# One language-model block on one core: the first sequence's six masked products in one group, its state share behind the turn of v, and GpSimd's copy of x's last columns behind the third addition

## What is computed

```python
h = emb[tokens] * sqrt(192) + position
u = rmsnorm(layernorm(h))
z, xBC, dt = split(u @ in_proj)            # 384, 512 and 24 columns
xBC = silu(conv4(xBC) + conv_b)            # causal, four taps over the tokens, per channel
x, B, C = split(xBC)                       # 384, 64, 64
dt = softplus(dt + dt_bias); decay = exp(-dt * exp(A_log))
S_t = decay_t * S_(t-1) + dt_t * x_t B_t   # per head, a 16 x 64 state
y = S_t C_t + D * x;  y = y * silu(z)
m = y @ out_proj;  v = rmsnorm(m)
h = h + m + (silu(v @ w_gate) * (v @ w_up)) @ w_down
x2 = layernorm(h)                          # the router takes two of eight experts
out = h + shared(x2) + sum_e cw_e * expert_e(x2)
```

## Time and profile before

| | |
|---|---|
| median of 3 runs | 796.38 us (795.68 to 796.73) |
| the profiled execution | 796.69 us, of which the span of the profile is 794.9 us |
| busy: PE, DVE, ACT, POOL | 757.6, 636.5, 546.8, 328.3 us |
| granted clock of PE | 0.991 of full over the span, full in the loop |
| one pass of the loop (first weighed sum of DVE at 389.85, then at 436.43) | 46.58 us |

### The profile page before, as it was taken

The page is one execution under the profiler, slowest core; times in us unless marked ns, Lnnn a source line. Parts: engine busy times, 40 slices in busy tenths (PEclk is TensorE's granted clock), DMA queues, the critical chain, the costliest instruction groups (busy, mean ns, idle before and its releaser), DMA issues.

```text
span 794.9 us, 23059 instructions
## 1 busy us (share of the span) xinstructions
PE 757.6 (95%) x7278; PEld 646.6 (81%) x7278; DVE 636.5 (80%) x1691; ACT 546.8 (69%) x1242; POOL 328.3 (41%) x478
## 2 busy tenths in 40 slices
PE   2679999999999999999999999999999999999897
PEld 1556788988888898888888888888988888888786
DVE  4699987879788787978878797887889788786745
ACT  4975777767777776777767677776767777675533
POOL 5355544433444443344344334434443443442222
PEclk9899999999999999999999999999999999999999
DMA  7420000000000000000000000000000000000000
GB/s 251 155 89 1 12 22 12 9 25 6 15 10 21 10 6 25 3 17 10 21 10 6 25 3 17 10 21 10 6 24 4 17 10 16 14 6 11 2 1 21
DMA packets 14923, 18.93 MB, mean 24 GB/s; under 512 B 4656, under 2 KB 13008, under 8 KB 14448
## 3 DMA queue, kind: packets, MB, share of 16 engines
q1 hardware_dynamic: 13264, 15.25, 6.0%
q0 software_dynamic: 1632, 3.34, 1.7%
HBM read 14.39 MB, written 4.19 MB: 23 GB/s over the span
## 4 chain that ended last, share of the span: by engine, by line
PE 87%; DVE 2%; issue 1%; ACT 1%; POOL 0%; DVEq 0%; POOLq 0%; ACTq 0%
PE bank L1554 40%; PE bank L1934 11%; PE bank L1862 8%; PE bank L1718 6%; PE bank L1707 5%; PE bank L1831 4%; PE bank L1818 3%; PE bank L1809 3%; PE bank L1795 2%; PE bank L1647 1%; PE bank L1652 1%; PE bank L1691 1%; DVE mr L1193 1%; PE bank L1901 0%; PE bank L1902 0%
## 5 line engine op out<-in xcount | busy, mean ns | idle before, releaser
L1193 DVE SCALAR_TENSOR_TENSOR mr<-er,gm 128x512 f32<-128x512 f32 x192 | 125.8, 692 | 4.1 <-ACT er L782 3.7
L782 ACT ACTIVATE er<-bank 128x512 f32<-128x512 f32 x192 | 106.0, 595 | 27.4 <-PE bank L1707 27.1
L1934 PE MATMUL bank<-w2t,w_raw 128*128 128x192 f32 x576 | 112.6, 327 | 0.4 <-DVE w_raw L1362 0.4
L872 ACT ACTIVATE sg<-bank 128x256 f32<-128x256 f32 x144 | 55.1, 382 | 61.8 <-PE bank L1554 50.9
L1132 DVE SCALAR_TENSOR_TENSOR xa<-xr,cw_,xa 128x256 f32<-128x256 f32 x192 | 92.4, 488 | 6.3 <-ACT xa L690 4.7
L1934 PEld LDWEIGHTS bank<-w2t,w_raw 128*128 128x128 f32 x576 | 91.0, 190 | 1.8 <-DVE w_raw L1455 0.7
L1554 PE MATMUL bank<-x_h,wt_lo 128*128 128x256 f16 x288 | 78.5, 273 | 0.0
L1554 PE MATMUL bank<-x_h,w_lo 128*128 128x256 f16 x288 | 78.5, 273 | 0.0
L1554 PE MATMUL bank<-x_l,w_hi 128*128 128x256 f16 x288 | 78.5, 272 | 0.0
L1554 PE MATMUL bank<-x_h,w_hi 128*128 128x256 f16 x288 | 78.4, 272 | 0.0
L1554 PE MATMUL bank<-x_h,wt_hi 128*128 128x256 f16 x288 | 78.4, 272 | 0.0
(11 more groups left out here) (239 smaller groups left out, 2197.3 us busy)
## 6 DMA issues: line engine op xcount, KB each, us to landing
out<-w_raw SPq DMA_DIRECT2D x16, 192.0 KB, 2.0
pos<-position SPq DMA_DIRECT2D x16, 96.0 KB, 1.9
ri<-exponent_rows SPq DMA_DIRECT2D x1, 1536.0 KB, 6.4
w_raw<-weights SPq DMA_DIRECT2D x1, 1156.0 KB, 6.0
wt_raw<-weights SPq DMA_DIRECT2D x1, 1156.0 KB, 8.4
sums<-lj SPq DMA_DIRECT2D x16, 64.0 KB, 1.9
w2t<-w SPq DMA_DIRECT2D x1, 864.0 KB, 11.6
w_raw<-weights SPq DMA_DIRECT2D x1, 768.0 KB, 8.1
```

The costliest lines, as they stand in the source:

```text
L782: act.activation(er[:, r % NER], p_d[r % 2][:].rearrange("p (h i) -> p h i", h=HG), ACT.Exp)\
L872: act.activation(sg[:, e % 4, :], src[e][:, 0:NB * Q], ACT.Silu).then_inc(sx_ready, 1)
L1193: ve.scalar_tensor_tensor(mr[:, r % NMR], er[:, r % NER], 1.0, gm[:, r // NQ, :].unsqueeze(1).to_broadcast([128, HG, Q]), ALU.min, ALU.mult)\
L1934: ins = pe.matmul(p_ex[e][:, b * D:(b + 1) * D], hh[:, e % NHH, b * Q:(b + 1) * Q], w2t[:, e, :], start=True, stop=True)
```

## The change

On PE, in `scan_front`: the exponents of unit 4 stand behind `skipped_x`; all six units of `masked` stand together; the turn of v follows, with the exponents of units 6 and 7 between its high and its low half, where `state_share` had been; `state_share` is last. On DVE, the mask of unit 5 stands ahead of v's low part. On ACT, the exponential of unit 5 stands ahead of v's high part. On POOL, the halo copy stands behind the third addition, not the first. No instruction is added or taken away, and none changes its size.

```diff
@@ POOL, experts(c, p), for e in range(NP)
-                    if e == 0 and p is not None:
+                    if e == 2 and p is not None:
                         halo(p)
@@ ACT, body (and finale alike)
-                    exponentials(f, range(6), {3: lambda: mixed(b), 5: lambda: mixed_norm(b)})
+                    exponentials(f, range(6), {3: lambda: mixed(b)})
+                    mixed_norm(b)
@@ DVE, body (and finale alike)
                     masks(f, range(5))
                     from_state(f, 0)
+                    masks(f, (5,))
                 v_low(b)
-                if f is not None:
-                    masks(f, (5,))
                 split_v(b)
@@ PE, scan_front(c, turned)
-                exponents(c, 4)
                 pe.wait_ge(eend_ready, c + 1)
                 pe.wait_ge(gm_ready, c + 1)
                 pe.wait_ge(bt_ready, c + 1)
                 for k in range(KT):
                     skipped_x(0, k)
+                exponents(c, 4)
                 state_read(c, 0, None)
                 exponents(c, 5)
-                masked(c, range(4))
-                exponents(c, 6)
-                turned(lambda: state_share(c, 0))
-                exponents(c, 7)
-                masked(c, (4, 5))
+                masked(c, range(NQ))
+
+                def last_exponents():
+                    exponents(c, 6)
+                    exponents(c, 7)
+
+                turned(last_exponents)
+                state_share(c, 0)
```

More of the change, by code:

```diff
@@ L899, in finale @@
             def finale(a, b):
-                exponentials(b, range(6), {3: lambda: mixed(a), 5: lambda: mixed_norm(a)})
+                exponentials(b, range(6), {3: lambda: mixed(a)})
+                mixed_norm(a)
                 split_v(a)
@@ L1394, in finale @@
                 from_state(b, 0)
+                masks(b, (5,))
                 v_low(a)
-                masks(b, (5,))
                 split_v(a)
```

## The result

The changed kernel takes **810.86 us** (median of 4 runs, 810.48 to 811.79) against 796.03 us (4 runs of the kernel before, 794.83 to 796.73): a ratio of 1.0194, with a 95% interval of 1.0179 to 1.0209. The profiled execution took 810.73 us, of which the span is 808.9; before it was 796.69 and 794.9. So the two profiles differ by 14.0 us.

What follows compares the result with a forecast made beforehand. The prediction took PE's own sequence as the bound. Experts' stage 7.1, loop fronts 7.8, the body before the loop about 0.7 and finale 0.6 made 16.2 us, giving 812.5 us; this case reaches 808 to 819, kept range 801 to 819.

Steps and rivals of the forecast that it cites:

- The bound: Whole kernel: PE's own work is 87% of the last-ending chain, so changes count by their effect on PE's sequence.
- DVE's taps and the lock: Experts' stage: POOL's additions block DVE's taps, third tap 1.01 us later, PE's transposes lose 0.51 per pass.
- What the POOL half gives to the front: Out projection in the scan's front: of the 0.47 us gain meant on DVE, only 0.06 is left.
- The sixth mask: Scan's front: mask ends at T + 6.83, PE idles some 0.8 us, MLP starts 0.60 later per pass.
- v's low part and t1: Scan's front on DVE: v's low part ready about T + 7.5, costing nothing; no wait for t1 before the share.
- The sum: Whole kernel: experts' stage 7.1, loop fronts 7.8, body before the loop about 0.7, finale 0.6; together 16.2 us.
- Pass each other: Experts' stage rival: additions and taps do not block each other; 803.4 us, range 800 to 807, chance 0.20.
- By recorded ends: Experts' stage rival: the lock holds until recorded ends, PE loses 1.21 per pass; 822 us, chance 0.05.
- Faster: Scan's front rival: no wait for the sixth mask opens, 0.73 us gained per pass; 787 us, chance 0.09.
- Nothing moves: Whole-kernel rival: savings repay PE's idle time at the sixth mask, slack covers the taps; about 796.5 us, chance 0.08.
- savings of "about 0.55": Scan's front on PE: reordering can remove about 0.55 us, one pair of switches and the wait for t1.

Runs made afterwards that it cites:

- POOL half alone: The kernel before with only POOL's halo copy moved behind the third addition; 801.36 us, ratio 1.0071.
- one addition alone: The kernel before with POOL's halo copy behind the second addition, so one addition runs beside DVE's taps; 795.32 us, ratio 0.9988.
- scan's half alone: The changed kernel with POOL's halo copy back behind the first addition, leaving only the reordered front; 806.19 us, ratio 1.0130.
- the copy last: The kernel before with POOL's halo copy behind the fifth addition, additions 2 and 3 held until DVE's last tap is done; 794.29 us, ratio 0.9987.
- the copy behind the third addition and the additions held: The kernel before with that halo copy place, POOL waiting for DVE's last tap ahead of its second addition; 794.64 us, ratio 0.9980.
- the grouping with the mask and v's low part brought forward: The scan's half alone with all six masks, then v's low part, then t1 on DVE, and unit 7's exponents behind v's turn on PE; 797.40 us.
- the one move on PE (unit 7): The scan's half alone with unit 7's exponents moved between the low half of v's turn and the state share; 803.48 us, ratio 1.0097.

## Why the prediction was right

It said 812.5 us, and the kernel took 810.86. Its terms, one by one:

- **The bound.** PE's sequence was the bound, and both halves of the change were paid there. It held.
- **DVE's taps and the lock.** Forecast: second tap +0.61, third +1.01. The pairs grew by 0.62 and 0.42, 1.04 in all. ACT's copy was to come 1.01 later and came 0.93 later; PE's transposes 0.51 forecast, 0.51 measured. The term holds, also in the run with the POOL half alone (0.54), but that it is exact has some luck in it: the copy's delay came out 0.08 smaller, since before it began 0.12 behind the last tap and now 0.03, and the step from the copy's end to the transposes was put at 0.1 to 0.15 and is 0.21. And it left out a wait. "The hidden product behind it reads PSUM and is only pushed along" is right for DVE (0.41 as before), but PE's next gate and up product waits for it, and loses 0.14 to 0.17 there. The transposes wait for a later moment anyway, so the sum does not change; with one addition alone this wait is what PE pays (0.17, where 0.1 was expected from the transposes).
- **What the POOL half gives to the front.** Forecast 0.06, measured 0.17 with that half alone, 0.16 in the pair. This is the term that was mis-sized. The step: "DVE's weighed sums +0.45 against PE's +0.51". `gm` came 0.95 later (from POOL's first addition, 10.58 before and 11.53 now), as forecast, but I let only the 0.47 of the earlier trace rows go from it. From the start of `gm` to the start of the weighed sums was 0.90 and is 0.34, so 0.56 went: the profile counts the wait from the recorded end of `gm` (0.42 behind its start), and without a wait the weighed sums start 0.08 before that end. They are 0.39 later against 0.54 of PE's exponents, and the 0.15 between is nearly the whole stall of the out projection (the exponents behind its first half stand 1.60 behind those of units 0 and 1 before, 1.43 now).
- **The sixth mask.** Forecast: it ends at T + 6.83; it ended at T + 6.73 (403.54; the forecast's T of 390.29 is the chain's row, 0.16 behind the timeline's 390.13, so that T is now 396.65 + 0.16 = 396.81). PE idle some 0.8 forecast, 0.64 in the timeline. The low turn was put at T + 7.78 and stood at T + 7.70, the MLP at T + 8.83 and T + 8.73. Each link is 0.08 to 0.10 early, which is the size of that one term. So the front costs 0.50, not 0.60. In the scan's half alone, where POOL gives nothing, it is 0.66; by the forecast's working it would have been 0.66 as well (0.60 + 0.06).
- **v's low part and t1.** "Costs nothing" for v's low part is right in the changed kernel, but only just: as soon as the mask came 0.47 earlier, it was next.
- **The sum.** 14 x 0.51 and 13 x 0.50 are 13.6. The body before the loop has the exchange too: from its first mask to ACT's copy of v 5.34 us before, 6.08 now, +0.74 against 0.7 forecast. But in the changed kernel's profile the ramp reached those masks 1.1 us earlier (62.92, before 64.05), so the MLP there starts 0.4 earlier instead of later. That is not the change: with the copy last, and with the copy behind the third addition and the additions held, all four engines have the instructions of before in the order of before up to 100 us, and yet reach the exponents of units 0 and 1 of that body at 59.61 and 61.47, where it was 60.65. The ramp's length differs by up to 1.9 us from execution to execution. The finale's front costs 0.43 (8.19 and 8.62), not 0.6. That makes 13.6 + 0.7 + 0.4 - 1.1 = 13.6 of the 14.0 measured. The other 0.4 lies right behind: the rest of the body before the loop is 0.70 longer, not 0.51 (40.54 us before, 41.24 now), and the first passes of the loop take up to 0.1 more than the later ones. Stage by stage the traces leave nothing open: ramp -0.86, 15 fronts 7.44, 14 rests 7.49, together 14.1. The medians differ by 14.8, and the forecast had 16.2. It put 9.1 on the fronts and 7.1 on the rests, which is 1.3 of the 1.4 between.

**The rivals.** *Pass each other* (803.4) needed taps of 0.48 each; the timeline shows the opposite. *By recorded ends* (822) would have the transposes 1.21 late. They were 0.51 late: the first addition ends at 387.80 + 1.17 = 388.97, and the second tap, whose pair ends at 389.25 and which takes 0.48, ran from 388.77, 0.20 before that end. Of the lock the Trainium skill, "SBUF — State Buffer", section "SBUF: two separate sides", says that the first to start has the port pair for the whole instruction; the rows agree on who waits for whom, but the waiting tap goes on 0.20 before the recorded end of the addition. *Faster* (787) needed the sixth mask before T + 6.1. The run with the sixth mask ahead of t1 has its unit at 6.63 (timeline), still with a wait. *Nothing moves* (796.5) holds for neither half; the nearest to it is the grouping with the mask and v's low part brought forward, 797.40. One sum in the prediction does not come out: the savings of "about 0.55" are, by its own rows, one pair of switches (0.30 + 0.32 - 0.43 = 0.19) and the wait for t1 (0.88 - 0.64 = 0.24), 0.43 together. The forecast's 0.60 is worked forward from T and does not use it; *faster* does, and would be 788 to 789 with it.

## What to carry to other kernels

When an instruction moves, look at what runs beside its new neighbours: two additions let out of an idle engine's queue made two of DVE's taps 1.0 us longer together, and cost three times what the wait they removed was worth (0.54 against 0.17 us per pass). When an instruction is delayed, follow everyone who waits for it, not only the last: PE met the delay first at the hidden product and then at the transposes. Before work is grouped on the engine that bounds, write down for each item when its input comes, because the last input now holds everything behind the group, and follow the next link (here v's low part, then t1) before counting on the first. Exchanges on the engine that feeds the bound are cheap to try: t1 ahead of the fifth mask took 0.08 us off the pass of the kernel before, and the sixth mask ahead of t1 took 0.21 off the scan's half, where the one move on PE (unit 7) took 0.17.

## What the runs showed of the hardware

- The lock between DVE and GpSimd shows as longer busy time, not as a wait: the taps' mean went from 488 to 562 ns with no more idle ahead of them (6.1 us, before 6.3). The busy time of DVE rose by 12 us (636.5 to 648.5) and looks like work. The hidden products, with one operand in PSUM, are not lengthened beside an addition (0.41 at 389.18).
- It lets go 0.20 us before GpSimd's recorded end, if the waiting tap itself takes its usual 0.48. The changed kernel shows it twice: the second tap from 388.77, against an end at 388.97, and the third from 389.92 (its pair ends at 390.79, less 0.39 and 0.48), against POOL's 390.12. The run with one addition shows it once more (383.06 less 0.48 is 382.58, against 382.78).
- One addition of 128x384 on GpSimd beside taps of 128x256 costs DVE 0.61 us, the second 0.42, and GpSimd itself 0.17 on one of two (1.17 against 1.00).
- The time from one engine's recorded end to the start of what waits for it on PE was 0.15 from the hidden product to the gate and up product (389.58 to 389.73, 383.39 to 383.54) and 0.05 from the sixth mask to the sixth unit (403.54 to 403.59).
- A small copy between two dependent additions on GpSimd costs nothing: 4.43 us for the four additions with it and without.
